# Per-patch expert weights by address from a pair table, and all three tap rows from DRAM

## The reference

```python
patched = patchify(x, PS)                    # (B*25, C, 10, 10)
feat = patched.mean(axis=(2, 3))
logits = feat @ Wg + bg
probs = jax.nn.softmax(logits, axis=-1)
routing = jax.nn.one_hot(jnp.argmax(logits, axis=-1), E) * probs
# expert: relu(conv(patched, w) + b); combined = einsum('ne,encij->ncij', routing, outs)
x = x + unpatchify(combined)[:, :, :H, :W]
```

## Time and profile before

| | us |
|---|---|
| three timed runs | 249.2, 249.26, 256.22 |
| median | 249.26 |
| the profiled execution: span from first to last instruction | 251.0 |
| PE busy / DVE busy / ACT busy / POOL busy | 186.8 / 166.2 / 131.6 / 15.7 |
| first convolution starts, last one ends | 38.8, 243.1 |

### The profile page before, as it was taken

One profiled execution on the slowest core, in us unless ns is written; L12 is line 12 of the kernel. 1 busy time (PEld: TensorE's weight loads), 2 busy tenths in 40 slices (PEclk: granted clock), 3 DMA queues, 4 the chain that ended last, 5 costly groups with the idle time before them and its releaser, 6 DMA issues.

```text
span 251.0 us, 12098 instructions
## 1 busy us (share of the span) xinstructions
PE 186.8 (74%) x5656; PEld 159.4 (63%) x5656; DVE 166.2 (66%) x348; ACT 131.6 (52%) x244; POOL 15.7 (6%) x23
## 2 busy tenths in 40 slices
PE   0002799689687978996999689998679984997650
PEld 0002577578576867785888578787568874887550
DVE  4873974944559866983579936985499749037335
ACT  2210495946455547663387518556565748469000
POOL 6600000010000000000000000001000100000000
PEclk9999999979957897598559955559977996599995
DMA  7677976990992729970894549770993499200202
GB/s 200 250 278 135 179 99 247 191 286 30 147 178 92 289 50 194 182 283 17 143 182 168 219 88 178 159 287 10 180 152 138 163 150 191 78 5 3 89 5 84
DMA packets 58069, 37.65 MB, mean 150 GB/s; under 512 B 53078, under 2 KB 53642, under 8 KB 56970
## 3 DMA queue, kind: packets, MB, share of 16 engines
q1 hardware_dynamic: 57300, 36.33, 65.8%
q10 hardware_dynamic: 336, 0.40, 0.4%
q0 software_dynamic: 384, 0.15, 0.4%
HBM read 21.89 MB, written 14.99 MB: 147 GB/s over the span
## 4 chain that ended last, share of the span: by engine, by line
issue 68%; DMA 12%; PE 12%; POOL 3%; DVE 2%; ACT 1%; DVEq 0%; SPq 0%; POOLq 0%
PE conv_bank L500 9%; DMA sums<-SUMS 9%; PE chunk_bank L489 3%; DMA XG<-wexp 2%; DMA FEAT<-sums 1%; POOL FEAT L163 1%; POOL XG L250 1%; DVE BLK L354 1%; DVE BLK L359 1%; POOL XG L244 1%; ACT XG L441 1%; DVE XT L363 0%; DVEq L61 0%; POOL sums L155 0%; DVE YT L348 0%
## 5 line engine op out<-in xcount | busy, mean ns | idle before, releaser
L500 PE MATMUL conv_bank<-XG,WS 97*32 97x64 f32 x4800 | 122.5, 255 | 29.7 <-issue 28.6
L500 PEld LDWEIGHTS conv_bank<-XG,WS 97*32 97x32 f32 x4800 | 102.2, 156 | 43.0 <-issue 33.6
L425 ACT COPY WS<-chunk_bank 97x500 f32<-97x500 f32 (+1 forms) x160 | 81.4, 568 | 57.4 <-PE chunk_bank L489 56.8
L489 PE MATMUL chunk_bank<-HOTT,WPF 128*128 128x100 bf16 x768 | 60.9, 236 | 2.2 <-DMA WPF<-weight_parts 2.2
L489 PEld LDWEIGHTS chunk_bank<-HOTT,WPF 128*128 128x128 bf16 x768 | 47.2, 113 | 12.9 <-issue 5.4
L348 DVE STREAM_TRANSPOSE YT<-conv_bank 128x320 f32<-128x320 f32 x40 | 20.1, 509 | 43.6 <-PE conv_bank L500 43.6
L431 ACT COPY XG<-XG 32x1400 f32<-32x1400 f32 (+1 forms) x48 | 41.3, 861 | 0.9
L293 DVE COPY WIND<-XN 128x500 f32<-128x500 f32 x40 | 24.0, 666 | 0.3
L302 DVE TENSOR_REDUCE SUMS<-WIND 128x25 f32<-128x2500 f32 x8 | 21.8, 2728 | 0.1
L464 PE MATMUL chunk_bank<-CONST,FEAT 100*32 100x100 f32 x8 | 2.3, 292 | 21.6 <-DMA FEAT<-sums 21.6
L341 DVE COPY XG<-XG 32x1400 f32<-32x1400 f32 (+1 forms) x32 | 16.8, 564 | 2.0 <-DMA XG<-windows 1.7
(11 more groups left out here) (41 smaller groups left out, 76.9 us busy)
## 6 DMA issues: line engine op xcount, KB each, us to landing
XG<-windows SPq DMA_DIRECT2D x16, 1000.0 KB, 12.3
windows<-WIND SPq DMA_DIRECT2D x8, 1250.0 KB, 5.9
XT<-x SPq DMA_DIRECT2D x8, 512.0 KB, 4.8
out<-XT SPq DMA_DIRECT2D x16, 256.0 KB, 2.5
weight_parts<-XG SPq DMA_DIRECT2D x1, 441.0 KB, 5.3
WPF<-weight_parts SPq DMA_DIRECT2D x1, 441.0 KB
CONST<-consts ACTq DMA_DIRECT2D x1, 384.0 KB, 5.1
XG<-wexp SPq DMA_DIRECT2D x1, 288.0 KB, 5.7
```

What stands on the lines that cost most here:

```text
L425: nc.scalar.copy(WS[g % 2][0:KC, t:t + n, :], chunk_bank[c % NCB][0:KC, 0:n * GN].rearrange("p (t n) -> p t n", n=GN)).then_inc(chunk_copi ...
L489: last = nc.tensor.matmul(chunk_bank[c % NCB][:, j * GN:(j + 1) * GN], wide(co, kx), HOTT[:], start=True, stop=True)
L500: last = nc.tensor.matmul(o, WS[g % 2][0:KC, kx * C:(kx + 1) * C, patch], taps, start=kx == 0, stop=kx == TAPS - 1)
```

## The change

- **Weights.** A table WP in SBUF holds, for each of the 64 ordered pairs of experts, the 192 weight columns of both side by side. It is laid out once, half by POOL and half by ACT, from a table `wtab` that comes from DRAM. For each patch position two images are a pair: a group has 50 pairs, of which ACT copies 25 and POOL 25 (`copies`), each a 128 x 192 float32 copy whose source address comes from a register. WS is a ring of 5 lots. The registers (25 for each of the two engines, a group) are loaded from a row of indices that a PE matmul and one DVE instruction make. The chunk matmuls, their copies, the bf16 parts and the warm-up matmuls are gone.
- **Taps.** All three tap rows come from DRAM: three DMAs a group instead of two, each of 32 x 100 runs of 320 bytes, row ky of channel c onto partition 4c + ky. Partition 4c + 3 holds ones (POOL fills both XG buffers at the start). The copies of the middle row are gone.
- **Routing.** The gate's product is taken on DVE from the window sums (PROD, GATE: a 128 x 400 multiply and a reduction) and summed by two small matmuls; sums no longer go through DRAM.
- **Windows.** The copy of the windows moves from DVE (five copies) to ACT (one instruction, 2500 elements a partition), placed after the first lot's copies of the next group.
- There are six PSUM banks for the convolutions instead of four.

The diff, cut to what the prediction speaks of:

```diff
+        WS = sb("WS", [128, RING, PAIRS, PAIR])
+        WP = sb("WP", [128, E * E * PAIR])
...
+        def pick_rows(engine, g, at, count):
+            return nc.values_load_multi_w_load_instructions(
+                IDX[g % 2][0:1, at:at + count], [engine.engine], min_val=0, max_val=(E * E - 1) * PAIR,
...
             def read_patches(g):
...
-                for ky, loaded in (0, first_tap_loaded[u]), (2, last_tap_loaded[u]):
-                    sp.dma_start(XG[u][ky * C:(ky + 1) * C],
...
+                for ky in range(TAPS):
+                    rows = bass.AP(XG[u], ky * GN * KROWS, [[ROWS * GN * KROWS, C], [KROWS, GN], [1, KROWS]])
+                    sp.dma_start(rows, windows_dram[u].rearrange("(n j) w -> j n w", j=C)
+                                 [:, :, ky * WIN:ky * WIN + KROWS]).then_inc(taps_loaded[u], 16)
...
         def _(pool):
+            def copies(g, lot, index):
+                at = g * LOTS + lot
+                if at >= RING:
+                    pool.wait_ge(conv_done, at - RING + 1)
+                for i in range(POOL_PAIRS):
+                    last = nc.gpsimd.tensor_copy(WS[:, at % RING, ACT_PAIRS + i, :],
+                                                 WP[:, bass.ds(index[lot * POOL_PAIRS + i], PAIR)])
+                last.then_inc(pool_copied, 1)
+            nc.gpsimd.memset(XG[0][:], 1.0).then_inc(ones_set, 1)
+            pool.wait_ge(table_loaded, 16)
+            nc.gpsimd.tensor_copy(bass.AP(WP, 0, [[E * E * PAIR, 128], [E * PAIR, E], [PAIR, E], [1, NW]]),
+                                  bass.AP(BLK, 0, [[H * W, 128], [NW, E], [0, E], [1, NW]])).then_inc(pairs_laid, 1)
+            nc.gpsimd.memset(XG[1][:], 1.0).then_inc(ones_set, 1)
+            pool.wait_ge(pairs_laid, 2)
+            for g in range(GROUPS):
+                pool.wait_ge(index_ready, g + 1)
+                index = pick_rows(pool, g, POOL_AT, LOTS * POOL_PAIRS)
+                for lot in range(LOTS):
+                    copies(g, lot, index)
...
             for g in range(GROUPS):
                 if g + 2 < GROUPS:
                     statistics(g + 2)
+                if g > 0:
+                    finish(g - 1)
                 if g + 1 < GROUPS:
                     routing(g + 1)
+                turn_lot(g, 0)
+                if g + 1 < GROUPS:
                     selection(g + 1)
...
         def _(act):
+            for g in range(GROUPS - 1):
                 if g + 2 < GROUPS:
                     root(g + 2)
+                exponent(g + 1)
+                act.wait_ge(index_ready, g + 2)
+                index = pick_rows(act, g + 1, 0, LOTS * ACT_PAIRS)
+                for lot in range(LOTS):
+                    copies(g + 1, lot, index)
+                    if lot == 0 and g + 2 < GROUPS:
+                        windows(g + 2)
...
         def _(pe):
             for g in range(GROUPS):
+                pe.wait_ge(taps_loaded[g % 2], 16 * TAPS * (g // 2 + 1))
+                for lot in range(LOTS):
+                    at = g * LOTS + lot
+                    pe.wait_ge(act_copied, at + 1)
+                    pe.wait_ge(pool_copied, at + 1)
+                    if at >= NCB:
+                        pe.wait_ge(lot_turned, at - NCB + 1)
+                    for n in range(lot * LOT, (lot + 1) * LOT):
                         last = conv(g, n)
+                    last.then_inc(conv_done, 1)
+                    if lot == 0 and g + 1 < GROUPS:
                         logits(g + 1)
+                    if lot == 2 and g + 1 < GROUPS:
+                        picks(g + 1)
```

More of the change, by code:

```diff
@@ L30, with build @@
 HALF = H * W // 2
[L33 to L58, removed]
+SEG = 2
+PAIRS = LOT * GI // 2
+ACT_PAIRS = 5
+POOL_PAIRS = PAIRS - ACT_PAIRS
+POOL_AT = 32
+INDICES = POOL_AT + LOTS * POOL_PAIRS
+RING = 5
+C_OWN, C_CODE, C_SPAN, C_HOME, C_PAIR, C_END = 0, 256, 264, 520, 720, 780
+def build(nc, x, wgs, bg, wtab, consts, out):
+    fp32, i32 = mybir.dt.float32, mybir.dt.int32
     ALU, ACT, AX = mybir.AluOpType, mybir.ActivationFunctionType, mybir.AxisListType
@@ L137, in build @@
         out_rows = out.rearrange("(g b) c h w -> g (b c) (h w)", b=GI)
[L139 to L164 removed]
+        def pick_rows(engine, g, at, count):
+            return nc.values_load_multi_w_load_instructions(
+                IDX[g % 2][0:1, at:at + count], [engine.engine], min_val=0, max_val=(E * E - 1) * PAIR,
+                skip_runtime_bounds_check_because="VectorE holds the index between 0 and the table's last pair")[1]
         block = ctx.enter_context(nc.Block())
@@ L397, in _ @@
                     normalise(g + 2)
-                    windows(g + 2)
-                turn_lot(g, 1)
-                if g + 2 < GROUPS:
-                    sums(g + 2)
-                turn_lot(g, 2)
-                turn_lot(g, 3)
-                if g + 1 < GROUPS:
-                    early_lots(g + 1)
-                turn_lot(g, 4)
+                for lot in range(1, LOTS):
+                    turn_lot(g, lot)
+                    if lot == 3 and g + 2 < GROUPS:
+                        gate(g + 2)
             finish(GROUPS - 1)
@@ L434, in _, with copies @@
+            def copies(g, lot, index):
+                at = g * LOTS + lot
+                if at >= RING:
+                    act.wait_ge(conv_done, at - RING + 1)
+                for i in range(ACT_PAIRS):
+                    last = nc.scalar.copy(WS[:, at % RING, i, :],
+                                          WP[:, bass.ds(index[lot * ACT_PAIRS + i], PAIR)])
+                last.then_inc(act_copied, 1)
             act.dma_start(CONST[:], consts).then_inc(small_loaded, 16)
-            act.dma_start(WGT[:], wg).then_inc(small_loaded, 16)
+            act.dma_start(WGS[:], wgs.rearrange("p (m k) -> p m k", k=NP)).then_inc(small_loaded, 16)
@@ L443, in _ @@
+            nc.scalar.copy(bass.AP(WP, NW, [[E * E * PAIR, 128], [E * PAIR, E], [PAIR, E], [1, NW]]),
+                           bass.AP(BLK, 0, [[H * W, 128], [0, E], [NW, E], [1, NW]])).then_inc(pairs_laid, 1)
             exponent(0)
-            for c in range(NCH):
-                chunk(0, c)
-            for g in range(GROUPS):
+            windows(1)
+            act.wait_ge(pairs_laid, 2)
+            act.wait_ge(index_ready, 1)
+            index = pick_rows(act, 0, 0, LOTS * ACT_PAIRS)
```

338 lines of the change are left out of this document (107 added, 231 removed).

## The result

The changed kernel takes **217.67 us** (median of four runs, 215.9 to 218.37); the kernel before, beside it, 251.5 (249.2 to 256.22). The ratio is 0.872, with a 95% interval of 0.862 to 0.882: 12.8% less time, where the forecast was 242 us. (The ratio compares means and leaves out two slower executions of the kernel before, 253.74 and 256.22 us.) The profiled execution took 215.9 us and has a span of 213.8 us, 37.2 less than before; this span lies 3.9 us under the median, where the one before lay 1.7 above its own.

What follows compares the result with a forecast made beforehand. PE set the old pace; SP's transfer loop was expected next. Third read at 64, four loops of 28.3, eighth read 200.4, landed 219.6, plus 16 and 7.9: 243.5, less 1.7 gives 242 us; range 196 to 258.

Steps and rivals of the forecast that it cites:

- forecast (A): Main case: reads stay at 175 GB/s, SP's transfer loop takes 28.3 us, kernel 242 us; chance 0.48, own range 233 to 254.
- rival B: Destination partitions limited the reads: 280 GB/s, three reads in 11.0 us, loop 22.2 us, kernel 200 us; chance 0.37.
- the nearest row is the steady one, and I take 175: Patch reads on the DMA queue keep the old steady 175 GB/s, so a third read adds 5.7 us to the loop.
- The small rise at the change-over: Between the old kernel's two reads the rate rose to 194 only; taken as evidence against a large gain from destination.
- I take 16 us: PE's time for a group without chunk matmuls, after the old last group's 15.6 us.
- The bound of 22.7 us: Upper bound for PE's group: 600 of the slow group's 704 matmuls, 26.6 x 600 / 704.
- the routing runs a group ahead, so this is worth nothing in the middle: Dropping the sums' way through DRAM shortens the routing path but gains nothing in middle groups.
- the chain on SP: SP's queue from first read's issue T: reads end T+18.2, stores land, load T+22.0, write lands, next read T+28.3.
- rival C: POOL becomes the bound: its 200 copies by register at 1.2 us each give 279 us; chance 0.15.
- their floor: Lowest time for one POOL weight copy, 0.16 us, from a plain fill at 0.85 ns a column.
- The break-even of C: POOL ends at 41 + 200p, passing the old 251 us at p = 1.05 us for a pair with its register load.
- The start: Before the loops: first convolution at 36 to 40 us, no gain on 38.8; third read at 62 to 66, taken 64.

Runs made afterwards that it cites:

- with blocks of 32: Changed kernel with each tap row sent to 32 neighbouring partitions, weight table's rows ordered to match; 249.82 us, ratio 0.983 to the kernel before.
- the two layouts inside one half: Changed kernel with each tap row on 32 neighbouring partitions (249.82 us), or on every second partition of one half (248.52 us).
- SP's new order: Changed kernel with windows made early, load of x behind stores of a group earlier, windows' write ahead of stores; 206.41 us, ratio 0.805 to the kernel before.
- the early windows: Changed kernel with normalisation, windows, gate and routing moved earlier on DVE and ACT, only their order changed; 214.38 us, ratio 0.848 to the kernel before.

## Why the prediction was wrong, point by point

| | forecast (A) | rival B | measured | with blocks of 32 |
|---|---|---|---|---|
| three reads, first to last packet, us | 17.1 | 11.0 | 12.9 | 18.2 to 18.8 |
| first convolution | 36 to 40 | 33 | 32.6 | 35.2 |
| third read issued | 64 | 58.8 | 56.72 | 62.08 |
| seventh read | 177.2 | 147.6 | 152.20 | 177.98 |
| eighth read | 200.4 | 164.7 | 171.88 | 202.69 |
| last convolution ends | 235.6 | 193.8 | 205.9 | 243.2 |
| from there to the span's end | 7.9 | 7.9 | 7.9 | 7.9 |

(B's end is 177.8 + 16.) The forecast's span of 243.5 us is 29.7 us too long. Of these, 17.7 us lie in the four loops from the third read to the seventh, 7.3 before the third read, 3.5 between the seventh and the eighth, and 1.2 behind it. The measured time, 217.67 us, lies inside the stated range of 196 to 258 and between A's 242 and B's 200. That 242 is missed by 24 us and not by 30 is luck: the text took 1.7 us off the span to get the median, where the measured median lies 3.9 us above its span.

- **The step that failed first: "the nearest row is the steady one, and I take 175".** The mean rate is 238 GB/s over the 12.9 us (273 to 310 in the lines shown), and the two layouts inside one half show that the destination is the reason. With blocks of 32, where the rate is near the one that was taken (164 to 169 GB/s on the mean), the third, seventh and eighth reads come within 2.3 us of the forecast. The small rise at the change-over was held against it, "though for a moment twice as many partitions are open". It was weak evidence: those two reads, to partitions 0 to 31 and 64 to 95, stand one behind the other in the queue, and most packets of that half-microsecond may still have gone to one of them (not shown). The reading of the lines was short, too: 148.25 to 159.5 leaves out the last packets, which end at 160.67. This step alone is 4.2 us in each of the loops.
- **The second: PE's group, "I take 16 us".** It takes 19.4 to 23.7 us in all but the last, and 18.2 there. The pauses of 1.16 us after each 128 matmuls were read the earlier trace rows and kept as a constant of the last group; but that group has the transfers at a share of 0.11, and the others run at 0.75. The bound of 22.7 us was in the text, and the measured groups lie near it by luck: it shares out busy time by the count of matmuls, and in the changed kernel 13.7 to 16.1 us of a middle group are busy and the rest is mostly pauses. In the changed kernel this error costs little, since SP's loop takes about as long (24 us). It shows once the loop is shorter: with SP's new order PE's groups of some 21 us set the pace.
- **Rival B** had the mechanism of the reads and still came to a span of 201.7 us, 12.1 short of the measured one. Its loops were 22.2 us, measured 23.9 on the mean: the reads took 12.9 us and not 11.0, and then in two loops the windows came some 2 us late from ACT, in the other two their write landed 6.6 and 7.1 us after its issue and not 5.9. That is 6.7 us over four loops and 5.3 more from the seventh read to the last group; PE's last group added 2.2, and the third read, 2.1 us earlier than B had it, takes that off again. (Its 200 us were the span less 1.7; the run has its span 3.9 under the median, which is the rest of its distance to 217.67.)
- **A wait left out.** Of the sums' way through DRAM, which falls away, the text said that "the routing runs a group ahead, so this is worth nothing in the middle". In the changed kernel the chain from windows to logits takes 7.1 us (96.91 to 104.03), and PE waits for it in three middle groups, 5.2 us in all (26.8 less the first 21.6). Taking these waits away with the early windows moved the time little (214.38 us, the intervals of the two ratios overlap). The trace has a reason: at the two long waits, which end at 80.34 and 104.03, the next instruction packet was still under way and ended at 80.98 and 104.67. The product and the sum take 1.2 and 0.6 us each, by the line view below, where the text had under 1 us for both.
- **Right: the chain on SP.** Reads, stores, their landing, load, write, reads: the order holds, and the new order, with the early windows, takes the kernel to 206 us. From the issue T the load of x comes at T+16.6 and the next read at T+24.2 (128.04, 144.66, 152.20), where the forecast had T+22.0 and T+28.3. PE's groups and this loop are nearly level: with the early windows alone PE waits for the reads, and the loop's 24 us set the pace.
- **Right: ACT and POOL are hidden, so rival C fell.** The groups by line:

```profile
L165 POOL COPY WS<-WP 128x192 f32 x200 | 60.1, 353 | 107.1 <-issue 93.5 <-PE conv_bank L395 13.5
L335 ACT COPY WS<-WP 128x192 f32 x200 | 52.1, 348 | 51.3 <-issue 43.7 <-PE conv_bank L395 7.6
...
L325 ACT COPY WIND<-XN 128x2500 f32<-128x2500 f32 x8 | 18.8, 2350 | 1.7 <-DVE XN L210 1.7
...
L221 DVE TENSOR_TENSOR PROD<-WGS,SUMS 128x400 f32<-128x400 f32 x8 | 9.3, 1163 | 0.3
...
L223 DVE TENSOR_REDUCE GATE<-PROD 128x16 f32<-128x400 f32 x8 | 4.6, 570 | 0.3
```

A copy by register takes 348 and 353 ns against the 0.35 us worked out for ACT, the windows 2.35 us against 2.3. Pieces of the chain put 25 register loads on ACT at 1.7 and 2.5 us a group (70 to 100 ns each), below the 5 us taken and below the 200 ns a load that the prediction cites from the Trainium skill. POOL's copies cost as much as ACT's and not the 0.16 us of their floor. The break-even of C, 1.05 us a pair, was never near. POOL held PE once, at the start.
- **The start was off, the end right.** The first convolution came at 32.6 instead of 36 to 40 and the third read at 56.72, outside its 62 to 66. The first three reads took 11.7 us (17.33 to 28.99) and not 17.1, so the convolutions waited for POOL's copies alone, for 5.9 us. From the last convolution to the end it is 7.9 us, as forecast.

## What to carry to other kernels

When a DMA runs with its engines' share full at little over half the rate of its first microsecond, the destination's partitions are the first thing to change: here reads spread over both halves of the partitions took 12.9 us for what 32 neighbours took in 18.2 to 18.8. When PE shows pauses after the same number of instructions each time that no semaphore explains, price a group by its instructions, not by its columns, and take the rate from a stretch with as many transfers beside it as the changed kernel will have. Where two chains are level, as PE's groups and SP's loop here, shortening one alone shows little (214.38 us beside 217.67, on two chips), and both together show the gain (206.41 beside 219.70, on one chip).

## What was not expected of the hardware

- PE's pauses follow a count of 256 instructions: 3.6 us a packet without other transfers, 4.5 us on the mean in the changed kernel (37 steps from 37.7 to 205.8). Halving the columns left the time as it was (219.77 us), and with twice the instructions the same convolutions took 36 us a group.
- A load of x and a write of the windows in a row (1.8 MB) put the next instruction packet 5.6 to 6.5 us behind the last; without the writes the longest step was 5.1 us.
- Whether the same pace set the kernel before was not tried: there PE showed 26.6 busy us of 27.9, and the 44 packets stood 4.8 us apart. A loop in place of the unrolled convolutions, which would make the instructions fewer in memory, was not tried either.
